# Loading and storing the expert layer's data four slices at a time

## The reference, cut to what matters

```python
def _L0_ffn_ref(x, controller, f1, f2, bias):        # x: (16, 2048, 1024)
    ne = controller.shape[1]                          # 16
    grouped = x.reshape(x.shape[:-2] + (-1, ne, d))   # groups of 16 tokens
    logits = jnp.einsum('...btd,des->...btes', grouped, controller)   # 16 x 4 slots
    tie = jnp.linspace(0.0, 1e-06, ne).reshape(ne, 1, 1)
    logits = logits + tie
    perm = (logits == jnp.max(logits, axis=-3, keepdims=True)).astype(x.dtype)
    sel = jnp.einsum('...btd,...btes->...besd', grouped, perm)        # one token a slot
    inner = jax.nn.relu(jnp.einsum('...besd,desf->...besf', sel, f1) + bias)
    inter = jnp.einsum('...besf,esfd->...besd', inner, f2)
    return jnp.einsum('...besd,...btes->...btd', inter, perm)
```

## Time and profile before

| | |
|---|---|
| runs without a profile | 6252.43 us (6246.36 to 6261.34, 3 runs) |
| profiled execution | 6254.24 us |
| its slowest core (4): span from the first to the last instruction | 6252.7 us |
| spans of the other cores | 6220.1 to 6239.4 us |
| PE / DVE / ACT / POOL busy | 33% / 33% / 14% / 3% of the span |
| DMA packets | 213305, of them 143280 under 512 bytes |

### The profile page before, as it was taken

How to read it: one execution, slowest core, us unless ns; L and a number is a source line. 1 busy time by engine, 2 the same in 40 slices (tenths; PEclk the granted TensorE clock), 3 DMA queues, 4 the chain that set the end, 5 groups by cost and what they waited for, 6 DMA issues and landing times.

```text
span 6252.7 us, 67766 instructions; the slowest of 8 cores (6220.1 to 6252.7 us)
## 1 busy us (share of the span) xinstructions
PE 2074.5 (33%) x28832; PEld 1265.8 (20%) x28902; DVE 2049.5 (33%) x2550; ACT 875.3 (14%) x931; POOL 196.7 (3%) x277
## 2 busy tenths in 40 slices
PE   2334334334334334343344332222222222222222
PEld 1231231231331331331331321111110011111100
DVE  2352352452442442442442443331111033311110
ACT  1101101101102102002002001111220011112200
POOL 0000000000000000000000000001110000011100
PEclk9556557556557557556556555555555555555555
DMA  4001000000000000000000000004444300044443
GB/s 69 1 1 34 1 1 34 1 1 34 1 1 34 1 15 20 1 15 20 2 29 6 1 23 9 9 9 59 67 64 96 119 9 9 9 56 67 66 97 118
DMA packets 213305, 189.21 MB, mean 30 GB/s; under 512 B 143280, under 2 KB 143376, under 8 KB 213008
## 3 DMA queue, kind: packets, MB, share of 16 engines
q0 software_dynamic: 149264, 42.24, 7.4%
q1 hardware_dynamic: 63744, 142.63, 6.8%
HBM read 168.24 MB, written 58.72 MB: 36 GB/s over the span
## 4 chain that ended last, share of the span: by engine, by line
PE 31%; DVE 26%; DMA 23%; ACT 9%; issue 8%; SPq 1%; DVEq 1%; ACTq 0%; POOLq 0%
DMA f<-f1w 7%; DMA f<-f2w 6%; PE psB L437 4%; DMA x1t_sb<-x1d 4%; DVE A L418 3%; DVE sel_sb L732 3%; PE psB L406 3%; PE psC L412 3%; DVE A L451 3%; DVE B L420 2%; PE pb L729 2%; PE psB L326 2%; PE psA L313 2%; PE psC L326 2%; DMA x_sb<-x 2%
## 5 line engine op out<-in xcount | busy, mean ns | idle before, releaser
L773 DVE CAST inter<-pb 128x1024 bf16<-128x1024 f32 x128 | 156.8, 1225 | 869.5 <-PE pb L766 869.5
L406 PE MATMUL psB<-A,B 64*64 64x64 bf16 x5120 | 272.9, 238 | 499.8 <-DVE B L420 395.7
L486 ACT ACT_TABLE_LOAD x64 | 82.1, 1283 | 2012.7 <-PE psC L481 2012.7
L406 PEld LDWEIGHTS psB<-A,B 64*64 64x64 bf16 x5120 | 256.1, 151 | 516.7 <-issue 516.7
L418 DVE CAST A<-psB 128x1024 bf16<-128x1024 f32 x160 | 195.9, 1224 | 389.2 <-PE psC L412 340.0
L754 PE MATMUL pb<-sel_sb,f 128*64 128x128 bf16 x1024 | 132.1, 310 | 508.3 <-DMA f<-f2w 508.3
L762 ACT ACT_TABLE_LOAD x128 | 164.2, 1283 | 849.5 <-PE pb L754 849.5
L738 POOL DMA_DIRECT2D f<-f1w x128 | 116.3, 908 | 5303.9 <-PE pb L729 4892.9
L326 PE MATMUL psB<-wk_sb,xn_fm 128*128 128x512 bf16 x504 | 180.3, 444 | 255.9 <-DVE kb_tm L354 246.0
L437 PE MATMUL psB<-A 64*64 64x64 bf16 x5120 | 170.1, 238 | 272.9 <-DVE A L451 218.4
L732 DVE CAST sel_sb<-pb 128x512 bf16<-128x512 f32 x256 | 177.0, 691 | 214.9 <-PE pb L729 201.5
(11 more groups left out here) (156 smaller groups left out, 4345.2 us busy)
## 6 DMA issues: line engine op xcount, KB each, us to landing
x_sb<-x SPq DMA_DIRECT2D x32, 1024.0 KB, 7.0
interd<-inter SPq DMA_DIRECT2D x128, 256.0 KB, 2.8
scat_sb<-interd SPq DMA_DIRECT2D x128, 256.0 KB, 4.1
x1t_sb<-x1d SPq DMA_DIRECT2D x64, 256.0 KB, 3.5
f<-f1w POOLq DMA_DIRECT2D x128, 128.0 KB, 3.6
f<-f2w POOLq DMA_DIRECT2D x128, 128.0 KB, 3.1
out<-outf_sb SPq DMA_DIRECT2D x32, 512.0 KB, 2.6
x1d<-x_sb SPq DMA_DIRECT2D x16, 512.0 KB, 3.6
```

The lines of the kernel that those rows point to most:

```text
L406: sq_fns.append(lambda t, k=k, h=h, par=par: t.matmul(psB[par:par + 64, h * 64:h * 64 + 64], B_bufs[k][par:par + 64, h * 64:h * 64 + 64], ...
L773: vI = E("v", [lambda v, ib=ib: v.tensor_copy(inter_sb[ib][:], pb3[:, 0:1024])], waits={"t": tF2, "y": em.cnt["y"]})
```

## The change

Four slots are now handled as one group j (16 groups in a half) wherever data move:

- `f1_load` and `f2_load` fetch four slots at once: 1024 pieces of 1 KB, and 256 rows of 4 KB. POOL issues 16 pairs of loads a half where it issued 64. The load of group j+1 waits for the last F2 of group j-1.
- The four results of a group are copied side by side into one `inter_sb` [128, 4096], and one store of 1 MB a group takes the place of four of 256 KB. The two buffers that `inter_sb` had are gone. `inter_d` has another layout, (e, R, k): the four rows that one partition needs in the scatter lie one behind the other, so the store writes 2 KB pieces at a pitch of 8 KB, in four blocks 2 MB apart.
- The scatter reads a tile's 1 MB with one transfer, in pieces of 8 KB, in place of four with pieces of 2 KB.
- To make room in SBUF, `scat_sb` shares its memory with an f1 buffer (`f1a`), `sqb_sb` with `yf_sb`, and `outf_sb` with both (`yfbuf`); the tie constants are stored once for 128 tokens, not for 4096.

What TensorE, ScalarE and VectorE compute stays the same, in the same order.

```diff
-            f1_sb = [pb.enter_context(nc.sbuf_tensor(f"f1_{i}", [128, 512], BF16)) for i in range(2)]
-            f2_sb = [pb.enter_context(nc.sbuf_tensor(f"f2_{i}", [64, 1024], BF16)) for i in range(2)]
+            f1a = pb.enter_context(nc.sbuf_tensor("f1a", [128, 4096], BF16))
+            f1_sb = [f1a[:, 0:2048], pb.enter_context(nc.sbuf_tensor("f1_1", [128, 2048], BF16))[:, :]]
+            f2_sb = [pb.enter_context(nc.sbuf_tensor(f"f2_{i}", [64, 4096], BF16)) for i in range(2)]
-            inter_sb = [pb.enter_context(nc.sbuf_tensor(f"inter_{i}", [128, 1024], BF16)) for i in range(2)]
-            scat_sb = pb.enter_context(nc.sbuf_tensor("scat_sb", [128, 4096], BF16))
-            outf_sb = pb.enter_context(nc.sbuf_tensor("outf_sb", [128, 1024], F32))
+            scat_sb = f1a
+            inter_sb = pb.enter_context(nc.sbuf_tensor("inter_sb", [128, 4096], BF16))
+            outf_sb = yfbuf[:, :].bitcast(F32)
...
-                def f1_load(g, es, buf):
+                def f1_load(g, j, buf):
                     return g.dma_start(
-                        out=f1_sb[buf][:, :].rearrange("p (c f) -> p c f", c=8),
-                        in_=f1_h[:, es * 64:(es + 1) * 64].rearrange("(c p) f -> p c f", p=128))
+                        out=f1_sb[buf].rearrange("p (c F) -> p c F", c=8),
+                        in_=f1_h[:, j * 256:(j + 1) * 256].rearrange("(c p) F -> p c F", p=128))
-                def f2_load(g, es, buf):
-                    return g.dma_start(out=f2_sb[buf][:], in_=f2_h[es * 64:(es + 1) * 64, :])
+                def f2_load(g, j, buf):
+                    return g.dma_start(
+                        out=f2_sb[buf][:, :].rearrange("p (el m) -> p el m", el=4),
+                        in_=f2_h[j * 256:(j + 1) * 256, :].rearrange("(el p) m -> p el m", p=64))
...
-                for es in range(64):
-                    buf = es % 2
-                    if es < 63:
-                        gF = E("g", [lambda g, es=es, buf=buf: f1_load(g, es + 1, 1 - buf),
-                                     lambda g, es=es, buf=buf: f2_load(g, es + 1, 1 - buf)],
+                for j in range(16):
+                    buf = j % 2
+                    if j < 15:
+                        gF = E("g", [lambda g, j=j, buf=buf: f1_load(g, j + 1, 1 - buf),
+                                     lambda g, j=j, buf=buf: f2_load(g, j + 1, 1 - buf)],
                                dma=True, waits={"t": em.cnt["t"]})
+                    for el in range(4):
+                        es = j * 4 + el
...
-                    vI = E("v", [lambda v, ib=ib: v.tensor_copy(inter_sb[ib][:], pb3[:, 0:1024])],
-                           waits={"t": tF2, "y": em.cnt["y"]})
-                    E("y", [lambda y, es=es, half=half, ib=ib: y.dma_start(
-                        out=inter_d[es * 256 + half * 128:es * 256 + half * 128 + 128, :],
-                        in_=inter_sb[ib][:])], dma=True, waits={"v": vI})
+                        E("v", [lambda v, el=el: v.tensor_copy(
+                            inter_sb[:, el * 1024:(el + 1) * 1024], pb3[:, 0:1024])],
+                          waits={"t": tF2, "y": em.cnt["y"]})
+                    E("y", [lambda y, e0=e0, kblk=kblk, half=half: y.dma_start(
+                        out=inter_d.rearrange("(e R k) m -> e R k m", e=16, R=256)[
+                            e0:e0 + 4, half * 128:half * 128 + 128, kblk, :].transpose([1, 0, 2]),
+                        in_=inter_sb[:, :].rearrange("p (el m) -> p el m", el=4))],
+                      dma=True, waits={"v": vI8})
...
                     ysc = E("y", [
-                        (lambda y, tl=tl, half=half, k=k: y.dma_start(
-                            out=scat_sb[:, k * 1024:(k + 1) * 1024],
-                            in_=inter_d.rearrange("(e R) m -> e R m", e=64)[
-                                k * 16:(k + 1) * 16,
-                                half * 128 + tl * 8:half * 128 + tl * 8 + 8, :]))
-                        for k in range(4)
-                    ] + [
+                        lambda y, tl=tl, half=half: y.dma_start(
+                            out=scat_sb[:, :],
+                            in_=inter_d.rearrange("(e R k) m -> e R (k m)", e=16, R=256)[
+                                :, half * 128 + tl * 8:half * 128 + tl * 8 + 8, :]),
```

## The result

The kernel after takes 5938.6 us (5934.1 to 5943.5, 8 runs), the kernel before 6256.9 (6246.4 to 6266.2, 8 runs): a ratio of 0.949 (95% interval 0.948 to 0.950). It is faster, but by 318 us where 468 were forecast, and 5938.6 lies above the range. The profiled execution took 5956.75 us. Its slowest core is core 0, with a span of 5955.2; all rows of after are of that core.

A forecast was written before the change was run, and what follows sets the result against it. The prediction took POOL's two expert loads, one behind the other, as the bound. From 6254.24 us it subtracted 398 for the experts and 70 for the scatter: 5786, stated as 5785; own range 5705 to 5870, widened to 5680 to 5905.

The forecast's parts named there:

- The pair alone: Expert stage: f1 and f2 loads of four slots, with two releases, take 12.6 us where four pairs took 32.
- The two landings taken from both sides: Expert loads: interpolated from smaller and larger transfers, f1 lands in 5.95 us and f2 in 5.55.
- The slot: Expert stage: with weights there, PE's computing sets a slot's length, 3.97 us where it was some 8.
- L - 4.1: Expert stage: PE's stall once a group if the store lands after L us; 2.9 taken, bounds 0.6 and 6.5.
- rival 1: Expert stage: TensorE's clock rises, up to 0.83 us less a slot, 106 us; time 5680; chance 0.14.
- Rival 4: Expert loads: landing grows with the bytes, about 31.7 us a group, slower than before; some 6280; chance 0.02.
- L = 1.3 + 32 x (0.106 + 0.073) = 7.0: Expert store: lands in 7.0 us beside the f1 load if the DMA engines take their pieces in turn.
- fixed 1.3: Expert store: some 1.3 us of the 4.7 that 1 MB takes alone do not depend on the pieces.
- Rival 2: Expert store: costs double at its new 8 KB pitch, landing in 10.4 us, stall 6.3; time 5895; chance 0.14.
- 4.9 + 0.5: Scatter: reads land after 5.4 us in place of 7.6, 70 us saved; bounds 0 and 2.7 us a tile.
- Rival 3: Scatter: reads at the 2 MB pitch are slower, 9.2 us in place of 7.6; time 5906; chance 0.09.
- 207 to 164 GB/s: Scatter: the skill's slowdown from 512 KB to 2 MB pitch; by it reads would take a fifth longer.

The follow-up runs named there:

- loadlate: Kernel after, with POOL's next pair of loads held back until the store has landed: 5852.5 us, 0.935 of the kernel before.
- oldlay: Kernel after, keeping the 1 MB store but with the old layout of inter_d and the old four scatter reads: 5898.2 us, 0.942 of the kernel before.
- vfirst: Kernel after, with the load also waiting for the group's last copy, so it is issued 0.5 us behind the store: 5837.4 us, 0.933.
- contig8k: Kernel after, with each tile's MB read from contiguous residual rows in one transfer of 8 KB pieces (output not the reference's): 5859.3 us, 0.936.
- best4: Kernel after, with two 512 KB stores a group, slots regrouped and kept in scatter order, 4 KB store pieces, linear tile read: 5758.4 us, 0.921.
- reklin: Kernel after, with inter_d as (R, e, k) and each tile's contiguous MB read in linear order (other slots' numbers are added): 5845.0 us, 0.932.
- scat4: Kernel after, with the new layout kept but a tile read in four transfers of 2 KB pieces: 5911.9 us, 0.946 of the kernel before.
- rek: Kernel after, with inter_d as (R, e, k): a tile's MB is contiguous, its pieces in another order than the partitions: 5909.2 us, 0.944.
- contig2k: Kernel after, with each tile's MB read from contiguous residual rows in four transfers of 2 KB pieces (output not the reference's): 5879.8 us, 0.940.
- rke: Kernel after, with inter_d as (R, k, e): the store writes 8 KB pieces, the tile is read in four transfers of 2 KB pieces: 5837.9 us, 0.933.

## Why the prediction was wrong

Two terms failed: the landing of the store beside the load, and the price of the scatter's read. What the rows bore out, step by step. The pair alone: 12.1 us against 12.6. The two landings taken from both sides: f1 5.8, f2 5.5 (loadlate), against 5.95 and 5.55. The slot: 3.99 against 3.97. PE waits for f2w only at the starts of the halves. DVE waits for the store once a group, 30 times, and PE's F2 for DVE behind it. The stall follows the prediction's L - 4.1: with 8.9 it gives 4.8, and half 1 has 4.6. The clock stays at 0.50: rival 1 did not come. Rival 4 did not come either.

**The step that failed in the experts** is "if the engines take them in turn, L = 1.3 + 32 x (0.106 + 0.073) = 7.0". They do take turns, and the turns were priced well: 117 and 122 pieces a us over 16 engines are 0.13 us a pair and engine at best, and over a whole store the 5.4 us from the first to the last piece are 0.17 a turn, for 0.179 forecast. But the turns begin late. The store, 0.9 us behind f1, moved its first piece 3.1 us after its issue (median) where it takes 0.9 by itself; the prediction's fixed 1.3 holds that and the last piece's landing. 3.1 + 5.4 + 0.4 is the 8.9 measured (the median of all cores), on core 0's half 0 it is 4.0 and 10.0. A stall of 2.9 became 4.6 and 5.9 beside a load: 18.8 us a group became 20.5 and 21.8. Rival 2 had the store dear (10.4) for another cause: neither the pitch of 8 KB (oldlay, 8.7) nor the store by itself (loadlate, 4.4) is dear. vfirst shows the cause, since exchanging the order alone brought 4.6.

**The step that failed in the scatter** is the price of one 8 KB-piece read, 4.9 + 0.5, taken from x loads of phase A. Those read one MB in one place, in the order of the partitions; the tile's MB lies in 16 blocks 2 MB apart. The price is right for a linear read (4.8 in contig8k and best4, and on six cores of reklin; tile 13.4) and wrong by 3.2 us for 16 blocks. So the bound of the term, 0 "(nothing but the shape changes)", left out the side that came: the tile lost 1.1 us. Rival 3 had the outcome (9.2, measured 8.6), but the distance alone isn't the cause: scat4, with the 2 MB and the old four transfers, starts PE after 7.5 to 8.0 us. The Trainium skill, "DMA: Bandwidth & Descriptors", section on latency and other measured facts, advises to pad the pitch by a few KB or to lay tiles out contiguously. The Trainium skill's figures there are for a pitch from one partition to the next; here only every eighth step is 2 MB. For this shape the runs differ on the first: 8 KB and 64 KB of padding brought the tile from 16.4 to 15.8 at best. On the second they agree only where the order is linear too: contiguous in another order is 15.45 (rek), linear 13.4 (reklin).

So of the 150 us that are missing, some 105 are the scatter's (70 forecast, 35 lost) and some 46 the store's (398 - 334, less the 18 of the one execution). Either alone would have left the time inside the range (5890 or 5831); the range took each rival by itself, and two came in part together. Both failed terms were durations borrowed from a transfer that ran in other company: one alone, one from one place. Two numbers of the prediction are off by themselves and change nothing: 207 to 164 GB/s makes a read a quarter longer, not a fifth, and the upper bound of the stall is 6.3, as in rival 2, not 6.5.

**Open.** Why order and spread matter is not settled. The runs show that busy engines deliver 180 to 270 GB/s across the blocks and 360 to 450 in linear order; which engine reads which block, and what in HBM would mind, no row shows. What keeps the store from starting while the engines are idle is open too. Nor is it known why cores 0 and 1 took 358 and 362 us in half 0. On core 0 the loads of that half moved their first piece 2.7 us after the issue (median), in its half 1 after 1.6; core 1 shows no such delay. It was no single event: in contig8k and contig2k cores 6 and 7 took 353 to 359 us in both halves.

## What to carry to other kernels

Here two transfers of two queues that started within a microsecond didn't share from the start: the one that got going first held the other back for 2 us and more. So let the one that the computing waits for go first, and give the other the cover. Before a landing is borrowed for a new read, compare not only bytes and piece size but where the pieces lie in HBM and in which order; a layout in which a transfer is one run, each partition's piece behind that of the partition before, was worth 2 to 3 us a MB here. One transfer in place of four won some 0.7 us a tile with it and lost 0.9 without. And when both ends of a term's range are drawn from one similar row, leave room on the other side of nothing, and ask what the time is if two rivals come together.

## What the runs showed of the hardware, unexpected

- A 1 MB store issued 0.9 us behind a 512 KB load moved its first piece 3.1 us after its issue (median; 1.9 to 4.6), by itself after 0.9; issued 0.5 us ahead, it landed in 4.6 us and the load in 9.0 in place of 5.8. Issued 0.2 us behind, it still went first, and 1.2 us behind, it waited for 895 of the load's 1040 packets.
- 1 MB in 8 KB pieces is read in 4.8 us in linear order (5.1 and 5.3 on two cores of reklin), 7.0 out of order within the same contiguous MB, and 7.7 from 16 blocks 2 MB apart, each in order, at equal packet counts.
- Where the blocks lie apart, four transfers of 2 KB pieces (PE starts after 7.5 us on most cores) beat one of 8 KB pieces (8.6). Where the MB is linear, it is the other way round (tile 14.0 to 14.7 and 13.4 to 13.8).
- Pieces of 8 KB in place of 2 KB brought a store's landing beside a load from 9.0 to 6.8 us (rke), by itself only from 4.0 to 3.8.
